# Layer-3 top-k attention: heads in pairs on row strips, a second score product with keys on partitions in place of transposes, and rewritten step orders

## The reference, cut to what matters

```python
def _L3_xattn_ref(x, knowledge_embeddings, Wq, bq, Wk, bk, Wv, bv, Wo, bo):
    # 16 heads of 8 features, TOP_K = 32
    Q = _split_heads(x @ Wq.T + bq)
    K = _split_heads(knowledge_embeddings @ Wk.T + bk)
    V = _split_heads(knowledge_embeddings @ Wv.T + bv)
    scores = jnp.einsum('bhsd,bhnd->bhsn', Q, K) / SCALE
    topk_scores, topk_indices = jax.lax.top_k(scores, 32)
    sparse_weights = jax.nn.softmax(topk_scores, axis=-1)
    context = jnp.einsum('bhsk,bhskd->bhsd', sparse_weights, V at topk_indices)
    return context @ Wo.T + bo
x = x + jnp.tanh(g_xattn[3]) * _L3_xattn_ref(_layernorm(x), ctx_1024, ...)
```

## Time and profile before

| | |
|---|---|
| median of 3 runs | 2767.58 us (2767.54 to 2768.53) |
| the profiled execution | 2768.71 us, span of its trace 2766.7 us |
| mean granted TensorE clock | 0.921 of 2.4 GHz |
| block ORDER_3_2, first of 4 | 416.0 to 575.4 us of the span, 159.4 us |
| block ORDER_3_0, first of 3 | 575.4 to 755.1 us, 179.7 us |
| block ORDER_LAST | 2579.0 to 2704.0 us, 125.0 us |
| the 8 blocks with wide attention | 1274.5 us together |

### The profile page before, as it was taken

The page is one execution under the profiler, slowest core; times in us unless marked ns, Lnnn a source line. Parts: engine busy times, 40 slices in busy tenths (PEclk is TensorE's granted clock), DMA queues, the critical chain, the costliest instruction groups (busy, mean ns, idle before and its releaser), DMA issues. The chain is left out here.

```text
span 2766.7 us, 41535 instructions
## 1 busy us (share of the span) xinstructions
PE 2435.2 (88%) x12585; PEld 1767.4 (64%) x12585; DVE 2075.0 (75%) x8036; ACT 1390.5 (50%) x3333; POOL 911.8 (33%) x1398
## 2 busy tenths in 40 slices
PE   5889988999989898989989979899998899889876
PEld 4555676676576567666657556657766666766655
DVE  1398978848696696967869679695777859798692
ACT  2435565744534456663543546566453355657441
POOL 3141213236234122424525221332542512142432
PEclk9889999989989989998999999998999899999888
DMA  5000000000000000000000000000000000000000
...
DMA packets 9069, 22.14 MB, mean 8 GB/s; under 512 B 642, under 2 KB 7810, under 8 KB 8066
## 3 DMA queue, kind: packets, MB, share of 16 engines
...
HBM read 18.28 MB, written 1.05 MB: 7 GB/s over the span
## 5 line engine op out<-in xcount | busy, mean ns | idle before, releaser
L182 DVE MATCH_REPLACE8 workQ<-top_eight,workQ 128x256 f32<-128x256 f32 x1664 | 667.2, 408 | 0.0
L184 DVE MAX8 top_eight<-workQ 128x8 f32<-128x256 f32 x1664 | 618.0, 413 | 0.3
L218 POOL TENSOR_TENSOR att_pQ<-att_pQ,top_rest 128x512 f32<-128x512 f32 x192 | 244.2, 1272 | 405.7 <-ACT top_rest L211 405.4
L489 PE MATMUL bank<-workP 128*128 128x256 f32 x1024 | 296.2, 414 | 7.2 <-ACT att_pP L201 3.9
L549 PE MATMUL bank<-att_pTP,att_vP 128*32 128x256 f32 x1024 | 265.2, 385 | 0.0
L666 DVE TENSOR_REDUCE att_nmaxP<-bank 128x2 f32<-128x512 f32 x256 | 175.1, 684 | 113.5 <-PE bank L489 113.3
L234 ACT ACTIVATE att_pTQ<-bank 128x512 f32<-128x512 f32 x192 | 115.3, 601 | 276.7 <-PE bank L112 276.6
L489 PEld LDWEIGHTS bank<-workP 128*128 128x128 f32 x1024 | 185.4, 200 | 89.0 <-issue 61.2
L201 ACT ACTIVATE att_pP<-bank,att_nmaxP 128x256 f32<-128x256 f32 x512 | 214.4, 475 | 40.0 <-DVE att_nmaxP L666 38.9
L628 POOL TENSOR_SCALAR workP<-workP,const 128x256 f32<-128x256 f32 x256 | 121.2, 478 | 274.2 <-PE bank L489 236.4
L234 ACT ACTIVATE att_pTP<-bank 128x512 f32<-128x512 f32 x256 | 153.8, 601 | 113.6 <-PE bank L112 112.8
...
## 6 DMA issues: line engine op xcount, KB each, us to landing
pack3w<-in_pack3w SPq DMA_DIRECT2D x1, 4608.0 KB, 20.5
...
pack<-in_pack SPq DMA_DIRECT2D x1, 2266.0 KB, 10.1
...
```

The source lines that it names most:

```text
L182: ins = nc.vector.match_replace(self.work[:, u % 2, j, :], eight, src, GONE)
L184: ins = nc.vector.max(eight, src)
L218: self.k.nc.gpsimd.tensor_tensor(v, v, self.rest[:, :, :], ALU.subtract).then_inc(self.p_ready, 1)
L489: mm = self.k.nc.tensor.matmul(self.banks[u % 2][:, j * T:(j + 1) * T], self.q1[:, u % self.RING, j * P:(j + 1) * P], self.kT, start=True, ...
```

## The change

Layer 3 gets a class of its own, `TopStripHeads`. Heads are taken in pairs. A head's queries are masked on a strip of 32 partitions (4 masks for the whole stage instead of one a head), and the products of the two heads of a pair go to different strips of 32 rows and to different banks, interleaved. ACT copies the scores of each head (128x512) into SBUF, and the four rounds of top-k work on the copy, where the 32 largest become a constant of -3e38. POOL makes a penalty of it with one add-and-multiply (about 0 where the score was among the 32 largest, -3e30 elsewhere), in bf16. The transposes and the subtraction are gone: PE computes the scores a second time with keys on the partitions, adds to them in the same bank the negative maximum of each query (three bf16 parts, made by five small operations on POOL, turned by PE, copied by ACT, and spread by a product with a constant) and the penalty, turned by a product with the identity. One exponential on ACT then gives what the product with the values takes. That product is issued for the two heads of a pair in turn, on two strips of columns. The order strings of all six kinds of block are rewritten.

```diff
+class TopStripHeads(Units):
+        self.units(3, H // 2, 2 * self.R, 5, 6)
...
+    def pe_scores(self, pe, u):
...
+        for j in range(NT):
+            for v in (u, u + 1):
+                r = self.strip(v)
+                mm = self.k.nc.tensor.matmul(self.banks[v % 2][:, j * T:(j + 1) * T], self.q1[r, v // NG, j * P:(j + 1) * P],
+                                             self.kT[r, :], start=True, stop=True)
...
+    def pe_maxima(self, pe, p):
+        pe.wait_ge(self.parts_ready, 5 * (p + 1))
...
+            tr = self.k.nc.tensor.matmul(self.banks[2][:, j * P:(j + 1) * P], self.parts[:, j, :], self.k.ident16[:, :],
+                                         start=True, stop=True)
...
+    def pe_turned_scores(self, pe, u):
+        if u + 2 < H:
+            pe.wait_ge(self.s_copied, u + 4)
+        pe.wait_ge(self.mT_ready, u // 2 + 1)
+        for kt in range(NT):
+            for v in (u, u + 1):
+                r = self.strip(v)
+                nc.tensor.matmul(self.banks[v % 2][:, kt * T:(kt + 1) * T], self.kT[r, kt * P:(kt + 1) * P], self.q1[r, v // NG, :],
+                                 start=(kt == 0), stop=False)
+        for v in (u, u + 1):
+            r = self.strip(v)
+            nc.tensor.matmul(self.banks[v % 2][:, :].rearrange("p (k t) -> p k t", k=NT),
+                             self.k.max_rows16[r, 0:1].broadcast_to([PAD, P]),
+                             self.mT[r, :].unsqueeze(1).broadcast_to([PAD, NT, T]), start=False, stop=False)
+        for v in (u, u + 1):
+            pe.wait_ge(self.pen_ready, v + 1)
+            for kt in range(NT):
+                for j in range(NT):
+                    mm = nc.tensor.matmul(self.banks[v % 2][:, kt * T + j * P:kt * T + (j + 1) * P],
+                                          self.pen[:, v % 2, j, kt * P:(kt + 1) * P], self.k.ident16[:, :], start=False,
+                                          stop=(kt == NT - 1 and j == NT - 1))
+            mm.then_inc(self.st_done, 1)
...
+    def act_scores(self, act, u):
+        for v in (u, u + 1):
+            act.wait_ge(self.scores, v + 1)
+            if v >= 4:
+                act.wait_ge(self.pen_ready, v - 3)
+            self.k.nc.scalar.activation(self.work[v % 4], self.banks[v % 2][:, :].rearrange("p (j t) -> p j t", j=NT),
+                                        ACT.Copy).then_inc(self.s_copied, 1)
...
+            for v in (2 * p, 2 * p + 1):
+                act.wait_ge(self.st_done, v + 1)
...
+                nc.scalar.activation(self.pT[v % 2], b[v % 2][:, :].rearrange("p (k t) -> p k t", k=NT),
+                                     ACT.Exp).then_inc(self.exp_done, 1)
...
+    def pool_penalty(self, pool, u):
+        pool.wait_ge(self.top, self.top_count(u, self.R - 1))
...
+        self.k.nc.gpsimd.tensor_scalar(self.pen[:, u % 2, :, :], self.work[u % 4], -GONE, -1.0e-8, ALU.add,
+                                       ALU.mult).then_inc(self.pen_ready, 1)
...
-        self.stages = [HeadAttention(k, "Q", 3, k.x[lane], k.ctxT[lane], k.psum[4:8], "a", topk=32, gate=3)]
+        self.stages = [TopStripHeads(k, "Q", 3, k.x[lane], k.ctxT[lane], k.psum[4:8], "a", 32, 3)]
```

More of the change, by code:

```diff
@@ L49 @@
 ORDER_FIRST = (
-    "QQQPPPPPQQQQQQQPQQPQQQQPPQQPPPPQPQQPPPPQQQQQPQPPPPQQQPQQPPPQPQQQPQQQPQPPQQPQPQPQPQQPPQQQPQQPQPQQPPQQQQPQPQQPPQ"
-    "QPPQQQQPPPQQQQPQQQQPQQPPQQ")
+    "QQQPPPPPPQQPPQQPQQQQQPQQPQPQQQPQPQQPQQQQQQPPPPQPPQPQPPQPQQPPQPQQQQPPQPPQQPQQPPQQQPQPQQPQPQQPPQQPQQQPPQQQPPQQPQ"
+    "QQQQPPQPPPQQQQPQQQQPQQPQPQ")
 ORDER_1_2 = (
-    "PQPPPQPQPQQPPQPQPQPPQPPPPQQPPQPQQPPQPQQPQPQPQPQQPQPQPQQPQQPQPQQPPQQPQPQPQPPPPPQQQQQPPPQQPPQPQQPPQPQQPPPQQQQQQP"
-    "PPQPPQPQPQQQQPQQPPQQPQQQQPPQQQQPPQQQPQPPQQ")
+    "QPQPPPPQPQPPPQPPQPQPPPPQQPPQPQPQQPQPPQPQQPQPQPQPQPQQPQPQQPQPQQQPPQQPQQQPPQPQPPQQQPPPQPQPPQPPQQQPQPPQQPQQPQPPQQ"
+    "PPPQQPQQQQQQPPPQQQPPQQQQQPPQQQQPPQQQPPPQQQ")
 ORDER_3_2 = (
-    "PQPQPPPQPQQPQPQPQPQPPQQPPPQQPPPQPQPPQQPQQPQPQPQPQPQQPQQPQQQQPQQPQQPPQQPQQPQQPQPQQQPPPPQQQQQPPPPQQQQPPQPQQPPQPQ"
-    "PQQPPPQQPPQQQPPQPQQQPPPQPPQPQQPQQPPPPQQP")
+    "PQPPPQPQPQQPPQQPPQPPQPPPQQQQPPPQPQQQPQPQPPQQPQPQPQPQQPQQPQPQPQQQPQQQPQPQQQPPQQPQPPPQQPQQQPPPQQPPPPQQQPPQPPQQQP"
+    "PQQQPPQQPPQQQQQQPPQPPQQPPQQQQPPPPQPPQQPP")
 ORDER_3_0 = (
-    "PQPPQQPPPQQPPQQQPPPPQQPQPPQQQQPQQQPQQQQPPQPPPQQPPPPPPQQPPPPPQQPQPQQQPPPQPQPQPQPQPQPQPPQPQPQPQQPPPPPPQPPQQQQQPP"
-    "PQQPPPPQPQPQPPQPQPQPPQQPQPPQPQQPQQPPQQQPPQPQPPQPQQPPQQQP")
+    "PQPPQPPQQQPPPQQQPQQPQQQPQQQPPQQPQQQPQPPQQQQQQPPQPPPQQPPPPPPPPQPPQPPQQQPQPPPPPQPQPPPPPPQQPPPPPPPPQPQQQQPQQQQQPP"
+    "PQPPQPPPQPQPPQQPQPQPQPQPQQPPPPPQPQQQQPPQQPQPPQQPQQPQPQQP")
 ORDER_1_0 = (
-    "QPQPPQPPPQQPQQQPPPPQQQQPQQQPQQQQPPPQQQQPPQQQQPQPPQQPQPQPPPPPPQQPPPQQQPPQPPQQPPQQPPPPPPPQQPQPQQPPPQPQQPPPQQQQQP"
-    "PPPPPQPQQPPPPPPPQPQPPQPPPPPQPPQPPQPQQQQPPQQPQQQPQQQPPPQQQQ")
+    "QPQPPQPPPQPQQQPQQQQPQQQPQPQQQQPQPQQQPQQQQQPPPQQQPPQPQPQPPPPPPPPQPPPQQQPPPPQQQPPQPPPPPPQQPPQQQPPPPQPQQQPQPPQQQP"
+    "PPPPPQPQQPPPPPPPPPPQQPPPQPQPQQPPPPQPQQQQQQPPQPQQPQQPPPQQQQ")
 ORDER_LAST = (
-    "PQPQPQPPPQQQPPQPQQQQQQQQQQPPQQQQQQQPQQQQQQQPPQQQQQQQQPQQPQQQPQQQQQPQQQQPQQQQQQQPQQQPQPPPPPPPQQQPQPQQQPPQQQQQQQ")
+    "PQPPQPQPPPQQQQQQQQQQQQQQPPQPQQQQQQQQQPQPPQQQQPQQQPQQQQQQQPPQQQQQQQQPPQQPPQQQQQQQQPQPQQPPPPQQPQQPQQPQQPPQQQQQQQ")
 def cols(pack):
@@ L667, in dve @@
                                         AX.X, ALU.max, negate=True).then_inc(self.max_ready, 1)
+        c = self.close(s)
+        if c == 2:
+            self.dve_normalise(dve)
+        if c == 5:
+            dve.wait_ge(self.out_ps, 1)
+            self.chain.link(dve, nc.vector.scalar_tensor_tensor(
+                out=self.x[:, :, :], in0=self.banks[3][:, 0:NT * D].rearrange("p (j d) -> p j d", j=NT),
+                scalar=self.k.tg[:, self.gate:self.gate + 1], in1=self.x[:, :, :], op0=ALU.mult, op1=ALU.add))
@@ L1664, in _ @@
                 nc.gpsimd.memset(wide_v[:, :, :, HD1:], 1.0).then_inc(preset, 1)
+                nc.gpsimd.memset(top_parts[:, :, :], 0.0).then_inc(preset, 1)
                 pool.wait_ge(preset, 1)
@@ L1709, in _ @@
                 nc.scalar.activation(k.part_rows16[:, :], k.w["part_rows"], ACT.Copy)
+                nc.scalar.activation(k.max_rows16[:, :], k.w["max_rows"], ACT.Copy)
                 act.wait_ge(g_ps, 1)
@@ L1765 @@
         "group_rows": np.kron(np.eye(HG, dtype=f), np.ones((PAD, 1), f)),
+        "strip_rows": np.tile(np.kron(np.eye(HG, dtype=f), np.ones((HD, 1), f)), (NG, 1)),
+        "max_rows": np.tile(np.concatenate([np.tile(np.eye(HG, dtype=f), (PARTS, 1)), np.zeros((PAD - PARTS * HG, HG), f)]), (NG, 1)),
         "part_rows": np.concatenate([np.tile(np.eye(E16, dtype=f), (PARTS, 1)), np.zeros((P - PARTS * E16, E16), f)]),
```

234 lines of the change are left out of this document (232 added, 2 removed).

## The result

The changed kernel takes 2780.98 us (median of 5 runs, 2780.49 to 2781.49), the kernel before, timed beside it, 2768.53 us (2767.54 to 2773.58). The ratio is 1.0042 with a 95% interval of 1.0027 to 1.0057: 12 us slower, where 23 us faster was forecast. The profiled execution took 2781.49 us, its span is 2779.7 us.

What follows compares the result with a forecast made beforehand. PE's queue was taken to bound ORDER_3_2 and ORDER_3_0, DVE's top-k ORDER_LAST. Terms of -16 us (four ORDER_3_2), -7 us (three ORDER_3_0) and 0 elsewhere took 2768.7 to 2746 us, range 2698 to 2798.

Steps and rivals of the forecast that it cites:

- The other eight blocks: Blocks other than ORDER_3_2, ORDER_3_0 and ORDER_LAST layer-3 terms: same instructions reordered, forecast 0, with 5 us either side.
- The granted clock: Layer-3 blocks: 0.96 and 0.92 before; the prediction called itself wrong if these changed, as no term held it.
- The sum of the seven layer-3 blocks: Four ORDER_3_2 at -4.0 us each and three ORDER_3_0 at -2.4 us each: -23 us in all.
- PE's work for a pair: Layer 3's pair of heads on PE: 4.94 us before, 4.76 us after (4.46 to 5.00).
- The penalty products: Turning the penalty on PE in layer 3: 128x128 bf16 products taken as 0.085 us apart, between 0.055 and 0.109.
- a visit to the row strips: PE switching to 32-row products and back in layer 3: 0.40 us extra each time.
- The waits: PE's stands in layer 3: relief of 2.8+1.4 us in ORDER_3_2, 2.2+1.2 in ORDER_3_0; block start adds 0.7.
- the second rival: Layer 3's products on different strips don't overlap: 2.8 us more a pair, about 2920 us; chance 0.05.
- The exponential of 512 columns: ACT's exponential in layer 3, two a pair of heads, priced at 0.685 us each.
- The wait of DVE for PE at the normalisation: Lane Q's result in ORDER_3_2: 20.2 us before, to shrink by about what the block loses.
- The new chain of lane Q: Rival: PE waits for the new penalty and maxima chain in layer 3, 1.0 us more a pair: 2802 us; chance 0.18.
- The relief is worth far more: Rival: 9 us a block go in ORDER_3_2 and 7 in ORDER_3_0, giving 2712 us; chance 0.22.

Runs made afterwards that it cites:

- one wait filled: Changed kernel plus six unread products in PE's queue ahead of the gelu experts' LayerNorm, in ORDER_3_2 only: 2767.74 us, ratio 1.0000.
- the last pair: Unread products at the long LayerNorm waits: changed kernel with old ORDER_1_2 and ORDER_1_0 strings, 2728.08 us; kernel before with its own waits filled, 2757.13 us.
- the filled run: Changed kernel with ORDER_1_2 and ORDER_1_0 strings of the kernel before, plus six unread products ahead of the gelu experts' LayerNorm in ORDER_3_2: 2740.60 us.

## Why the prediction was wrong, step by step

**The steps that failed.** There are two, and the forecast named both as what would make it wrong.

- "The other eight blocks ... have the same instructions in another order; I have no row that favours either order and take 0, with 5 us to either side." They moved by +18.5 us, and putting two old strings back with one wait filled on both sides gave 18.9 us again. ORDER_1_0's new string costs 3.3 us a block: at the same clock (0.92) and the same busy time PE stands 21.2 us in it instead of 17.6. In the run with the old class and new strings PE stands just as long (22.1 us), which a higher clock hides there (0.94, busy 153.37 us, 175.4 us in all); and where the old string took 177.9 us, it was the clock. ORDER_1_2's new string is slower in every run: 624 to 627 us in four, where the old string took 610 to 621 us; with the waits filled on both sides it is 3.0 us a block. Of the +3.2 us of its first copy 1.5 us are time in which PE stands and 1.7 us busy time at a lower clock, and that copy did not get shorter when only its own string was put back (154.8 us behind the new ORDER_FIRST), so how it splits between the string and what runs ahead of it is not shown.
- The granted clock, "which no term here holds". ORDER_3_2 fell from 0.96 to 0.87. Filling one wait of 2.76 us gave back 4.6 us a block there, with the same work behind the wait the low clock stayed, and together with the old wide strings ORDER_3_2 took 154.6 to 157.4 us where 155.4 was forecast.

**The sum of the seven layer-3 blocks** would have been about right with the long waits filled on both sides: -17 us measured by the last pair against -23. But that is luck, since it comes out by two errors that cancel:

- PE's work for a pair was overpriced: 4.76 us. The rows give 0.96+0.32+0.45+1.07, 0.12 for the maxima's turn, 0.99 for the values, and 0.16 in the two products behind the strips (0.92 and 0.96 for 0.86): 4.07 us, read at one place each. The penalty products start 0.056 us apart (0.45 us for 8), the lower bound and not the 0.085 taken, let alone the 107 ns of a weight load, and a visit to the row strips costs 0.16 and 0.31 us, not 0.40. In the first ORDER_3_2 of the run that filled one wait and had the old wide strings, at a clock of 0.95, PE's busy time without the unread products (2.9 us) is 138.6 us, 5.7 less than the 144.3 of the earlier trace rows where I had -0.5.
- The waits were not relieved: -4.2 and +0.7 us were forecast for ORDER_3_2, -3.4 and +0.7 for ORDER_3_0. In ORDER_3_0 PE stands 13.9 us where it stood 14.0; in ORDER_3_2 13.1 where it stood 15.1, with a slower PE. Lane Q's own waits went in ORDER_3_2, as the table of waits shows: 3.5+2.1 us before, now 1.2 and 1.0 us. But lane P's took their place. The changed kernel in its first ORDER_3_2 (total, times, longest):

```profile
PE bank L112 <- DVE yP L259: 5.0, 2, 2.8
...
PE bank L759 <- POOL workQ L955: 1.2, 1, 1.2
PE bank L783 <- ACT top_mT L916: 1.0, 1, 1.0
```

 The same first line stood at 2.3 us in the kernel before. In that block of the filled run PE is free of own work for 154.6-138.6 = 16.0 us, where it was 159.4-144.3 = 15.1 us. The forecast asked what lane Q waits for, and not what lane Q's small pieces had covered for lane P.

**The steps that held.** The strips run together, so the second rival falls. DVE's work in ORDER_3_2 stayed (123.9 for 125.1 us), ACT's fell to 85.65 us (forecast 85), ORDER_LAST is at 125.4 us. The exponential of 512 columns took 0.598 us, not 0.685. The wait of DVE for PE at the normalisation shrank from 20.2 us to 16.6 us, although the block, to which the forecast had tied it, became 2.9 us longer:

```profile
DVE att_rdenQ L864 <- PE bank L112: 16.6, 1, 16.6
```

**The rivals.** The new chain of lane Q is not what PE waits for: 1.0 us before the second scores and nothing before the penalty in ORDER_3_2. Only in ORDER_LAST does it show (5.5 us before the next pair's scores, six times), where DVE leads and it costs nothing. "The relief is worth far more" would have been closest for ORDER_3_0, -5.9 us a block, but not by its mechanism: what went is PE's busy time (5.6 us, at 0.94 for 0.92) and not its idle time. With waits filled on both sides it is -1.3 us a block, and between the two rows at 0.94 -2.1 us (173.90 and 176.00). In the old class ORDER_3_0 itself came down from 179.7 to 176.0 us when other blocks were filled, with PE's busy time 2.4 us shorter at 0.94, so a part of the -5.9 us is the clock and none of the class.

The Trainium skill (TensorE: Matmul & The Clock Gate, What's actually happening) says that the default is the throttled clock and that activity releases it. The trace agrees in that the clock fell when PE went idle and stayed up when that time was filled. It shows no quick return with activity, since PE was busy 15.24 of the 18 us at 0.53, and one fall without idle time (524.7 us, with one wait filled).

**What stays open** is what sets the length of a stretch at the lower clock. PE stands 4.4 us in ORDER_1_0 for a LayerNorm in the kernel before and in the changed one alike (4.39 us until 866.72, 4.40 us until 863.02); then follow 14 us at 0.77 in the one and at 0.55 in the other, though PE is busy in both (61 records pass in the one, 46 in the other). Before, then changed:

```profile
866.70:880.70 14.00, 13.65 (x61) 10.85 (x62) 8.96 (x36) 6.11 (x15) 3.63 (x8) 0.77 0.00 1
```

```profile
863.00:877.00 14.00, 13.80 (x46) 11.18 (x47) 7.77 (x34) 3.94 (x10) 2.80 (x6) 0.55 0.00 0
```

So the idle time does not set the length of the low stretch by itself; over the whole block the two come to the same mean, 0.92. Open is, too, why one and the same ORDER_1_2 takes 151.3 us in one place and 154.8 us in another of the same execution, and the old string of ORDER_1_0 175.0 or 177.9 us. The clock's mean differs (0.92 and 0.91, 0.92 and 0.89), the instructions don't, and the blocks ahead of them do; what of these decides was not isolated. Block lengths are read from one execution of each kernel, and ORDER_FIRST (137.0 and 141.6 us) shows that a difference of a few us in one block need not come from the program.
